# A graph layer on one core: 24 dense batches, builds of six matmuls split by nodes, and own rows kept by the head

## The reference

```python
h = jnp.maximum(_layernorm(x, axis=-1), 0.0)
parts = [jax.nn.relu(h)]
for t in range(3):
    msg = jax.nn.relu(h[src] @ W_e[t].T + b_e[t])
    msg = jnp.where((edge_type == t)[:, None], msg, 0)
    parts.append(segment_sum(msg, dst, num_segments=6250))
agg = jnp.concatenate(parts, axis=1)                  # 6250 x 512
updated = agg @ W_n[t].T + b_n[t]  for t = node_type  # by node
out = x + (updated + h)
```

## Time and profile before

| | us |
|---|---|
| median of 3 runs | 1807.21 |
| the profiled execution | 1800.96 |
| its span, first to last instruction | 1798.9 |
| TensorE busy | 1524.0 |
| VectorE busy | 1050.5 |
| ScalarE busy | 579.9 |
| GpSimd busy | 1127.5 |

### The profile page before, as it was taken

How to read it: one execution, slowest core, us unless ns; L and a number is a source line. 1 busy time by engine, 2 the same in 40 slices (tenths; PEclk the granted TensorE clock), 3 DMA queues, 4 the chain that set the end, 5 groups by cost and what they waited for, 6 DMA issues and landing times.

```text
span 1798.9 us, 27966 instructions
## 1 busy us (share of the span) xinstructions
PE 1524.0 (85%) x9634; PEld 1201.8 (67%) x9634; DVE 1050.5 (58%) x3510; ACT 579.9 (32%) x1129; POOL 1127.5 (63%) x1076
## 2 busy tenths in 40 slices
PE   6956888888898968888989888877888889999887
PEld 2444777677677756767767676656777677777774
DVE  7564556556556666656565555566565556656542
ACT  5652333223233243223323323243322323332320
POOL 0067677767667675767676776675666656667560
PEclk9977889899989888989888998988899899999997
DMA  5442111111111221111111111222111111111120
GB/s 202 150 113 58 45 43 48 48 49 45 48 48 46 67 78 51 48 46 47 49 46 46 44 48 45 68 71 55 46 49 49 46 47 49 52 48 51 48 52 15
DMA packets 78936, 103.64 MB, mean 58 GB/s; under 512 B 19894, under 2 KB 58965, under 8 KB 78795
## 3 DMA queue, kind: packets, MB, share of 16 engines
q0 software_dynamic: 33920, 69.54, 14.8%
q1 hardware_dynamic: 43997, 31.29, 5.6%
q10 hardware_dynamic: 878, 1.02, 0.2%
HBM read 88.96 MB, written 12.80 MB: 57 GB/s over the span
## 4 chain that ended last, share of the span: by engine, by line
PE 60%; DVE 14%; issue 11%; another core or an unknown queue 9%; ACT 4%; DVEq 1%; ACTq 0%
PE ps L569 24%; PE ps L555 15%; PE ps L541 8%; DVE arena L1002 5%; PE ps L592 4%; DVE lhot L1004 3%; PE ps L488 3%; DVE acc L986 2%; PE ps L590 2%; ACT arena L726 2%; DVE xr L1041 1%; DVE work L1026 1%; ACT mem L737 1%; PE ps L486 1%
## 5 line engine op out<-in xcount | busy, mean ns | idle before, releaser
L437 POOL DMA_INDIRECT rows<-message_table,idx x1060 | 1123.8, 1060 | 626.1 <-issue 284.0
L726 ACT CAST arena<-ps 128x500 f16<-128x500 f32 x828 | 446.0, 580 | 1010.4 <-PE ps L555 552.4
L569 PE MATMUL ps<-mem,arena 128*120 128x384 bf16 x3381 | 702.3, 351 | 69.7 <-issue 55.5
L569 PEld LDWEIGHTS ps<-mem,arena 128*120 128x120 f16 x3381 | 472.7, 145 | 200.4 <-issue 98.2
L555 PE MATMUL ps<-arena,lhot 128*128 128x200 bf16 x3312 | 452.4, 288 | 45.9 <-issue 32.2
L1002 DVE TENSOR_SCALAR arena<-iota_j,jkey 128x400 bf16<-128x400 f16 (+1 forms) x1656 | 460.8, 339 | 4.9 <-remote 4.8
L986 DVE TENSOR_TENSOR acc<-ps,acc 128x20 f32 (+1 forms) x679 | 131.4, 193 | 564.8 <-remote 304.7
L555 PEld LDWEIGHTS ps<-arena,lhot 128*128 128x128 bf16 x3312 | 346.6, 111 | 109.8 <-issue 67.1
L541 PEld LDWEIGHTS ps<-onehot,rows 128*128 128x128 f32 x2120 | 282.5, 201 | 62.1 <-issue 57.0
L541 PE MATMUL ps<-onehot,rows 128*128 128x27 f32 x2120 | 275.7, 269 | 52.2 <-issue 32.8
L1004 DVE TENSOR_TENSOR lhot<-iota_l,lkey 128x512 bf16<-128x512 f16 x414 | 281.1, 679 | 0.0
(11 more groups left out here) (109 smaller groups left out, 412.4 us busy)
## 6 DMA issues: line engine op xcount, KB each, us to landing
rows<-message_table,idx POOLq DMA_INDIRECT x1060
message_table<-work SPq DMA_DIRECT2D x48, 192.0 KB, 1.8
work<-message_table SPq DMA_DIRECT2D x18, 448.0 KB
xr<-in_x_dram SPq DMA_DIRECT2D x48, 64.0 KB
out_dram<-xr SPq DMA_DIRECT2D x48, 64.0 KB
work<-message_table SPq DMA_DIRECT2D x3, 384.0 KB
arena<-in_L_gnn_W_n_dram ACTq DMA_DIRECT2D x1, 768.0 KB, 9.7
acc<-in_src_dram SPq DMA_DIRECT2D x3, 256.0 KB
```

The costliest lines, as they stand in the source:

```text
L437: pool.indirect_dma_start(out=rows[:, g % SLOTS, u, :], out_offset=None, in_=table_rows, in_offset=bass.IndirectOffsetOnAxis(ap=idx[:, g, ...
L569: m = pe.matmul(psQ[q % 2][0:BG * WG, 0:3 * D], counts[q % 2][:, c * MC + e, :], planes[:, c * MC + e, :, :].rearrange("p v d -> p (v d)") ...
L726: act.copy(counts[q % 2][:, half * HH:(half + 1) * HH, k * WG:(k + 1) * WG], psB[m % 4][:, 0:HH * WG].rearrange("p (h w) -> p h w", w=WG)) ...
```

## The change

It does five things. (1) One more batch is dense: 24 batches in place of 23, so 72 batch passes, 432 builds and 504 products in place of 69, 414 and 483, and 259 gathered groups in place of 265; the loop has 265 steps in place of 271. (2) A build's two PSUM buffers are split by destination in place of source: each holds all 50 rows and 10 of the 20 destinations. A quarter of the edges only touches the buffers that its window reaches, so a build takes 3+3 matmuls of 400, 350, 50, 50, 300 and 450 columns in place of eight of 200, 200, 175 and 225. ScalarE's casts keep their 500 elements. (3) The head keeps the blocks' own rows. GpSimd adds h to x there, and SyncE stores x+h (in four pieces) and the transposed h (one of 64 KB for each block) to HBM. At a block's end two loads bring them back; the normalization, the transposition, its copy and VectorE's addition there are gone. (4) `turn_slots` stands behind all pieces of its step, where it stood behind the first. (5) `dense_add` stands right behind the step's `add`, where it stood at the end of the step.

```diff
-BATCHES = 23
+BATCHES = 24
-HH = HB // 2
+WH = WG // 2
+    own_x = nc.dram_tensor("own_x", [NB * P, D], F32, kind="Internal").ap()
+    own_hT = nc.dram_tensor("own_hT", [NB, D, P], F32, kind="Internal").ap()
+        KEPT = (0, 13, 26, 38, NB)
...
@@ SyncE, the head @@
             for i in range(NB):
+                sp.wait_ge(hT_ok, i + 1)
+                sp.dma_start(own_hT[i, :, :], hT[:, i % UN, :]).then_inc(hT_out[i % UN], 16)
+                if i + 1 in KEPT:
+                    a = KEPT[KEPT.index(i + 1) - 1]
+                    sp.wait_ge(xh_ok, i + 1)
+                    sp.dma_start(own_x[a * P:(i + 1) * P, :].rearrange("(b p) d -> p b d", p=P),
+                                 xb[:, a * D:(i + 1) * D].rearrange("p (b d) -> p b d", d=D)).then_inc(xh_out, 16)
                 sp.wait_ge(tab_msg[i % UN], i // UN + 1)
...
@@ SyncE, load_x @@
-                sp.dma_start(xr[0:n, j % 4, :], x[i * P:i * P + n, :]).then_inc(x_ld[j % 4], 16)
+                sp.dma_start(xr[0:n, j % 4, :], own_x[i * P:i * P + n, :]).then_inc(x_ld[j % 4], 16)
+                sp.dma_start(hT_own[:, j % 4, :], own_hT[i, :, :]).then_inc(hT_ld[j % 4], 16)
@@ GpSimd, the head @@
+            for i in range(NB):
+                pool.wait_ge(h_ok, i + 1)
+                pool.tensor_tensor(xb[:, blk(i)], xb[:, blk(i)], h[:, i % UN, :], ALU.add).then_inc(xh_ok, 1)
@@ TensorE, count @@
-                    to = psB[m % 4][:, 0:HH * WG].rearrange("p (h w) -> p h w", w=WG)
-                    for u in range(TPG):
-                        a = JAT[u] + half * HH * WID[u]
-                        t = pe.matmul(to[:, :, OFF[u]:OFF[u] + WID[u]], lhot[:, i % HOTS, u, 0:P],
-                                      jhot[:, i % HOTS, a:a + HH * WID[u]],
-                                      start=(u == 0), stop=(u == TPG - 1), skip_group_check=True)
+                    to = psB[m % 4][:, 0:HB * WH].rearrange("p (h w) -> p h w", w=WH)
+                    at = half * WH
+                    tiles = [u for u in range(TPG) if OFF[u] < at + WH and OFF[u] + WID[u] > at]
+                    for u in tiles:
+                        a, z = max(OFF[u], at), min(OFF[u] + WID[u], at + WH)
+                        by_node = jhot[:, i % HOTS, JAT[u]:JAT[u] + HB * WID[u]].rearrange("p (h w) -> p h w", w=WID[u])
+                        t = pe.matmul(to[:, :, a - at:z - at], lhot[:, i % HOTS, u, 0:P],
+                                      by_node[:, :, a - OFF[u]:z - OFF[u]],
+                                      start=(u == tiles[0]), stop=(u == tiles[-1]), skip_group_check=True)
...
@@ TensorE, finish and the loop @@
-                pe.wait_ge(own_st, j + 1)
+                pe.wait_ge(hT_ld[j % 4], 16 * (j // 4 + 1))
+                if j >= 1:
+                    pe.wait_ge(fin_ok, j)
...
-                for j in fin_at(s):
-                    own_transpose(j)
                 for kind, i in pieces(s)[:1]:
...
-                for q in turns_of(s):
-                    turn_slots(q)
                 for kind, i in pieces(s)[1:]:
...
+                for q in turns_of(s):
+                    turn_slots(q)
@@ ScalarE, the head and the loop @@
             def norm(i):
+                if i >= UN:
+                    act.wait_ge(xh_ok, i - UN + 1)
...
             def copy_t(i):
                 if i >= 4:
                     act.wait_ge(tab_mm, i - 3)
+                    act.wait_ge(hT_out[i % UN], 16 * (i // UN))
...
-                for j in fin_at(s):
-                    own_copy(j)
                 for kind, i in pieces(s):
...
-                for j in fin_at(s + 1):
-                    own_norm(j)
@@ VectorE, the loop @@
                 if s < NS:
                     add(s)
-                for j in fin_at(s):
-                    own(j)
+                for q in adds_of(s):
+                    dense_add(q)
                 for j in fin_at(s - 1):
                     finish(j)
...
-                for q in adds_of(s):
-                    dense_add(q)
```

More of the change, by code:

```diff
@@ L217, in build @@
         st = [work[:, a * MC * D:(a + 1) * MC * D].rearrange("p (h d) -> p h d", h=MC) for a in range(2)]
-        h_own = work[:, 4 * TD + 4 * D:4 * TD + 6 * D].rearrange("p (s d) -> p s d", s=2)
-        hT_own = work[:, 4 * TD + 6 * D:4 * TD + 8 * D].rearrange("p (s d) -> p s d", s=2)
+        hT_own = work[:, 4 * TD + 4 * D:4 * TD + 8 * D].rearrange("p (s d) -> p s d", s=4)
+        fb_h_own = work[:, 0:D]
+        fb_hT_own = work[:, D:2 * D]
         xr = sb("xr", [P, 4, D])
@@ L285, in build @@
         o_st = [sem(f"o_st{i}") for i in range(4)]
-        own_h = sem("own_h")
-        own_add = sem("own_add")
-        own_t = sem("own_t")
-        own_st = sem("own_st")
+        xh_ok = sem("xh_ok")
+        xh_out = sem("xh_out")
+        hT_out = [sem(f"hT_out{i}") for i in range(UN)]
+        hT_ld = [sem(f"hT_ld{i}") for i in range(4)]
         fin_mm = sem("fin_mm")
@@ L364, in _ @@
                 sp.dma_start(table[i * P:i * P + n, :], msg[0:n, i % UN, :]).then_inc(tab_out[i % UN], 16)
+            for s in range(UN):
+                sp.wait_ge(hT_out[s], 16 * len(range(s, NB, UN)))
+            sp.wait_ge(xh_out, 16 * (len(KEPT) - 1))
             for s in range(UN):
@@ L577, in turn_slots, with finish @@
                              ident[0:BG * WG, 0:BG * WG]).then_inc(d_turn, 1)
-            def own_transpose(j):
-                pe.wait_ge(own_h, j + 1)
+            def finish(j):
+                i = ORDER[j]
+                pe.wait_ge(hT_ld[j % 4], 16 * (j // 4 + 1))
                 if j >= 1:
                     pe.wait_ge(fin_ok, j)
-                pe.transpose(psF[:, TD:TD + P], h_own[:, j % 2, :], ident[:, :]).then_inc(own_t, 1)
-            def finish(j):
-                i = ORDER[j]
-                pe.wait_ge(own_st, j + 1)
                 pe.wait_ge(acc_add, THROUGH[READY[i]])
                 pe.matmul(psF[:, 0:TD], ones[:, :], bn_3[:, :], start=True, stop=False)
-                pe.matmul(psF[:, 0:TD], hT_own[:, j % 2, :], wnT[:, 0, :], start=False, stop=False)
+                pe.matmul(psF[:, 0:TD], hT_own[:, j % 4, :], wnT[:, 0, :], start=False, stop=False)
                 for t in range(T):
@@ L602, in _ @@
                     finish(j)
-                for j in fin_at(s):
-                    own_transpose(j)
                 for kind, i in pieces(s)[:1]:
+                    if kind == "build":
+                        count(i)
+                    else:
+                        product(i)
+                for kind, i in pieces(s)[1:]:
                     if kind == "build":
@@ L611, in _ @@
                     turn_slots(q)
-                for kind, i in pieces(s)[1:]:
-                    if kind == "build":
-                        count(i)
-                    else:
-                        product(i)
             rest = pe.value_load(flag[0:1, 0:1], min_val=0, max_val=1)
@@ L632, in _ @@
                     pe.wait_ge(fb_h, i + 1)
-                    pe.transpose(psF[:, TD:TD + P], h_own[:, 0, :], ident[:, :]).then_inc(fb_t, 1)
+                    pe.transpose(psF[:, TD:TD + P], fb_h_own, ident[:, :]).then_inc(fb_t, 1)
                     pe.wait_ge(fb_hT, i + 1)
                     pe.matmul(psF[:, 0:TD], ones[:, :], bn_3[:, :], start=True, stop=False)
-                    pe.matmul(psF[:, 0:TD], hT_own[:, 0, :], wnT[:, 0, :], start=False, stop=False)
+                    pe.matmul(psF[:, 0:TD], fb_hT_own, wnT[:, 0, :], start=False, stop=False)
                     for t in range(T):
@@ L725, in counted @@
                     act.wait_ge(d_build, m + 1)
-                    act.copy(counts[q % 2][:, half * HH:(half + 1) * HH, k * WG:(k + 1) * WG],
-                             psB[m % 4][:, 0:HH * WG].rearrange("p (h w) -> p h w", w=WG)).then_inc(d_count, 1)
+                    at = k * WG + half * WH
+                    act.copy(counts[q % 2][:, :, at:at + WH],
+                             psB[m % 4][:, 0:HB * WH].rearrange("p (h w) -> p h w", w=WH)).then_inc(d_count, 1)
             def split(m):
@@ L1028, in plane_rests @@
                 dve.tensor_tensor(planes[:, to, 2, :], st[m % 2][:, :, :], planes[:, to, 1, :], ALU.subtract).then_inc(m_low, 1)
-            def own(j):
-                dve.wait_ge(own_h, j + 1)
-                dve.tensor_tensor(xr[:, j % 4, :], xr[:, j % 4, :], h_own[:, j % 2, :], ALU.add).then_inc(own_add, 1)
             def finish(j):
                 i = ORDER[j]
-                dve.wait_ge(own_add, j + 1)
+                dve.wait_ge(x_ld[j % 4], 16 * (j // 4 + 1))
                 dve.wait_ge(fin_mm, j + 1)
```

21 lines of the change are left out of this document (5 added, 16 removed).

## The result

The changed kernel takes 1732.68 us (median of 4 runs, 1724.42 to 1736.42), the kernel before 1806.16 us in the same comparison (4 runs, 1801.04 to 1811.46). The ratio is 0.9587, with a 95% interval of 0.954 to 0.9634: some 73 us faster. The forecast was 1779, with 1730 to 1828 as its range. The direction was right; the gain was 2.6 times the 28 us that the sum had.

A forecast was written before the change was run, and what follows sets the result against it. It took TensorE's work and waits to bound the kernel. From the profiled 1801.0 us, +39 - 34 - 14 - 5 - 18 + 4 = -28 gave 1773, or 1779 us as a median; range 1730 to 1828.

The forecast's parts named there:

- What bounds the kernel: In the loop, TensorE sets the time by its work and waits; GpSimd's gathers, some 1410 of 1650 us, are near.
- The work, +39 us: TensorE's added products and builds, less groups and transpositions, plus 0.83 us a build: +35.5 us, +39 at clock 0.905.
- The own-row waits, -34 us: TensorE's waits at transposing own rows at block ends: two thirds of 50.6 us come back, between 0 and -51.
- The turn -14: Moving a batch's turn behind all pieces of its step gives back 14 of 23.4 us waited, between 0 and -23.
- the additions -5: Dense additions moved ahead on VectorE save 5 us, from -10 to +20, against 10.2 us of first-product waits.
- The head, +4 us: Before the loop, extra stores and GpSimd additions mostly fit beside the table stores: +4 us, from 0 to +35.
- the third rival: The head pays: stores of transposed h and the pieces hold back the table, 1807 us; chance 0.12.
- the cover of three blocks: In the head, 3.7 us of slack before ScalarE's next write of h covers a GpSimd addition waiting out VectorE.
- the prediction's -22 us: Alternative builds term: a floor of about 62 ns per short matmul makes a build 0.76 us, -22 in place of +9.
- The second rival, cheap builds: A build's excess goes with its eight short matmuls: 0.68 us a build, 72 us below the forecast, 1707 us; chance 0.08.
- The clock, -18 us: Fewer falls to 1.2 GHz after the 17 normalization waits: a third of 54 us, from 0 to -54.
- The first rival, waits only move: Waits at transposition and turn reappear at the next group, added batch paid in full; put at 1830 us, chance 0.20.

The follow-up runs named there:

- the light products: The kernel before with three of each product's seven matmuls: 1742.67 us (0.9749) beside 1782.8 us; 1541.39 us in one run beside 1556.0 us.
- three gathers: The kernel before with three of a group's four gathers, the fourth quarter reusing the first's rows: 1528.29 us (0.855).

## Why the prediction came out as it did

**What bounds the kernel: half right.** TensorE does, in the profile. But that its work "sets the time" did not hold: an eighth of it was paid, by the light products. And GpSimd "is near, but not the bound" and gathers that "bounded nothing" missed what they do to TensorE. The rows were there: `issue` at 11% of the chain, and 8.92 us of idle with no named cause. I took that for an oddity of one place; beside it lay 128.8 us of TensorE's idle time with nothing waited for, and with three gathers the 342 us at the lower clock are 131.

**The sum, term by term.** For TensorE it had +39 of work and -18 by the clock, so +21 of busy time; measured are +2. It had -34, -14 and -5, so -53 of idle time; measured are -78, of which 39 are waits with a name and 39 idle time with nothing waited for, a term that the sum put at nothing.

**The work, +39 us: the step that failed.** It took TensorE's work as paid in full. The form of the builds was even priced too low: 0.88 us and not 0.83, 432 x 0.05 = 22 us more, so nearly +60 us by the same arithmetic. TensorE's busy time rose by 2 us instead. The clock gave back 36 of that; the other 20 us are open, since busy time rests on modelled ends. The 24th batch alone was priced at 23.9 + 14.6 - 5.3 us, some +37 at the mean clock, and measured -15 us (0.9913) where the ends are late and -10 us where they are not. The missing term is the 24 gathers, put down at nothing: by the three gathers each is worth 0.96 us here, 23 us. That leaves +14 and not -15. By an estimate, the other 29 us are the work, which was priced as paid in full: at the light products' eighth, the batch's 33 us cost 4 and the sum is some -19, inside the measured -9 to -22. Both prices come from much larger edits. The batch also takes away 6 groups with 48 fp32 matmuls and 6 additions of VectorE that wait for word of their ends; what they give wasn't tried by itself.

**The own-row waits, -34 us, between 0 and -51: too large, inside its range.** With the 4 us of the head and 7 us of transpositions that is -37; alone it gave -20 (-8 to -32), so some -17 for the waits. The wait went to zero as said. The clock did not move with it (0.906), so the share of the -18 us that was put there fell. What came back did so as idle time with no name, and not at the next group's sums, which grew by 2 us.

**The turn -14, the additions -5: right.** -19 together, measured -25 (-12 to -37). The turn's wait, 10.1 us, is under the 12 us that was named. L541 on additions rose from 18.3 to 27.0 us, under the 40.

**The head, +4 us: no loss.** SyncE's first load behind the head, before at 103.57 us:

```profile
99.25 0.55 SPq L402 DMA_DIRECT2D xr<-own_x  x1
```

The DMA share of the head is 0.77 where 0.70 was expected; the third rival needed it to bind, and it didn't. Of the additions on GpSimd there most are short, and some are not:

```profile
29.39 2.27 DVE L888 SCALAR_TENSOR_TENSOR rows<-acc 128x2048 f32<-128x2048 int32 x1
...
30.18 1.80 POOL L448 TENSOR_TENSOR arena<-arena,work 128x128 f32<-128x128 f32 x1 [1.77 <-ACT work L683]
32.40 0.45 POOL L448 TENSOR_TENSOR arena<-arena,work 128x128 f32<-128x128 f32 x1 [0.42 <-ACT work L683]
```

The mean is 0.637 us over 49, above the 0.39 us of the upper bound, the median 0.454. The long one began beside an instruction of VectorE with two SBUF inputs and ended at 31.98 us, 0.32 us behind that one's end. The rule of the Trainium skill, "SBUF — State Buffer", section on the shared port pair, that one waits the other out, agrees with that; the cover of three blocks held, as the prediction had it.

**The builds and the floor of the Trainium skill** ("TensorE: Matmul & The Clock Gate", the section on the 56 ns gap): the page gives its 62 ns for one way of decoding matmuls only, which the prediction left out. The first short matmul of a build, 0.059 us, agrees with it, the second, 0.092, doesn't; and the prediction's -22 us by it did not come, since those of 300, 350 and 450 columns take 0.037, 0.021 and 0.032 us above 0.424 ns a column. The second rival, cheap builds, is out.

**The clock, -18 us (0 to -54): mis-sized.** It gave some 36 us, and 59 at most if the idle time is counted in. It did not follow from the waits at own rows or at the turn: 0.906 and 0.903 with either edit alone, against 0.905. It rose where the idle time with nothing waited for fell: 0.911 with the builds alone (98.2 us of it), 0.923 with 24 batches (66.0 us) in the group at 1782.8 us, where the kernel before has 0.904 to 0.912.

**The first rival, waits only move,** was the right suspicion with the wrong outcome: the late ends are real, and half of what own rows gave back did move. But it is not a fixed delay for each end, by which the added batch would be paid in full; it depends on the gathers, and the change has fewer.

The parts' ratios multiply to 0.9887 x 0.9864 x 0.9971 x 0.9913 = 0.964, against 0.9587 (0.954 to 0.9634): they about add up within their intervals, and no interplay between them is needed.

**What stays open:** how the gathers make TensorE's ends late, and why the same kernel has it in three groups of runs and not in the two others, once on the same chip. That its instructions or their completions are held up by the gathers' traffic is only a guess, and the gathers' packets, 0.126 us each with and without late ends, don't speak for it. Nor do the gathers bring late ends by their number alone: in the traces of the groups at 1554 and 1556 us all four a group go out in less time, and there are no remote waits. No version clearly faster than the changed kernel was found; 23 batches or the old builds are within 1.2% of it, and more than 24 weren't tried.

## What to carry to other kernels

When the profile shows idle time of the bounding engine that waits for nothing, and others' waits with no releaser, add them up before any edit is priced: here an edit that took them away, one gather in four left out, was worth a seventh of the time. Work moved from the gathers to TensorE can pay even where the profile shows TensorE as the bound and GpSimd idles. And where one kernel's time differs by some 15% between groups of runs, the same change is worth 4% in one and 0.6% in another, so both are to be stated.

## What the runs showed of the hardware

- The same kernel took 1554 to 1556 us in two groups of runs and 1783 to 1807 us in three, each within 1.6%, with a clock of 0.90 to 0.91 in the slower ones and of 0.95 to 0.96 in the faster ones.
- With all four gathers of 1.06 us a group, TensorE stood idle 128.8 us for nothing the profile shows, and ScalarE and VectorE waited 689 us for releases that it can't place. With one gather in four left out these were 9.0 and 74 us, and the kernel took 0.855 of its time. With a fill of 0.97 us on GpSimd in its place they stayed away (8.8 and 1.4 us).
- That fill slowed VectorE: a one-hot instruction of 400 columns took 0.499 us in place of 0.326.
- ScalarE acted on half a build 5.6 us behind the modelled end of its last matmul (the ninth of ten, in the kernel before), so a TensorE that is idle in the profile may be one that had not finished; that was not shown.
- A matmul of 450 columns in runs of 9 cost 0.223 us at full clock, where one of 400 in runs of 8 took 0.169; the first is always the last of its build, so its place may have a part in it.
